# A graph network on one core: padding slots spread over rows, last stage unrolled and its side work moved

## What is computed

```python
x = x + gnn0(layernorm(x), edges, edge_attr)     # per edge: relu(W1 . [x_src, x_dst, attr]); summed per source node
x = x + experts(layernorm(x))                    # shared MLP + top-2 of 4 experts
# two SAGE layers on xn = layernorm(x):
h      = relu(mean_neighbours(xn) @ W_l1 + b1 + xn @ W_r1)
logits = mean_neighbours(h)  @ W_l2 + b2 + h  @ W_r2
x = x + logits
# last block: only the rows with the highest routing weight get the MLP
xn      = layernorm(x)                           # "XN" / "y" in the kernels
weights = xn @ wr + br
top     = the k-1 highest weights (k = half of the 3125 rows, ties by index)
mlp     = gelu(xn @ w1 + b1) @ w2 + b2           # 256 -> 1024 -> 256
x       = x + xn + where(row in top, mlp * weight, 0)
```

## Time and profile before

| | |
|---|---|
| median of the timed runs | 3331.05 us (3328.54 to 3333.71, 3 runs) |
| the profiled execution, its own time | 3306.88 us |
| its span, first to last instruction | 3304.9 us |
| mean granted TensorE clock | 0.865 of 2.4 GHz |
| busy, share of the span | PE 78%, DVE 59%, POOL 55%, PE weight load 44%, ACT 23% |
| DMA | 401.32 MB, mean 121 GB/s |

### The profile page before, as it was taken

The page is one execution under the profiler, slowest core; times in us unless marked ns, Lnnn a source line. Parts: engine busy times, 40 slices in busy tenths (PEclk is TensorE's granted clock), DMA queues, the critical chain, the costliest instruction groups (busy, mean ns, idle before and its releaser), DMA issues. The chain is left out here.

```text
span 3304.9 us, 33972 instructions
## 1 busy us (share of the span) xinstructions
PE 2592.2 (78%) x8449; PEld 1445.8 (44%) x8449; DVE 1966.1 (59%) x4316; ACT 773.9 (23%) x2022; POOL 1819.5 (55%) x1847
## 2 busy tenths in 40 slices
PE   4487784199999899879999877777777777777598
PEld 1133331055544444446666644433334343443476
DVE  7999996377776667514333644444435444444768
ACT  1001010277666666522232300000001000000132
POOL 3777777476665556412100067777754777777310
PEclk8788897599999999989999977788868877777799
DMA  9222220499999999961110033333343333334311
GB/s 256 68 69 82 61 81 13 149 264 263 255 239 234 221 235 234 189 163 49 40 39 9 13 106 105 105 105 105 106 89 101 106 106 105 105 105 103 86 50 41
DMA packets 198569, 401.32 MB, mean 121 GB/s; under 512 B 44315, under 2 KB 93230, under 8 KB 198064
## 3 DMA queue, kind: packets, MB, share of 16 engines
q0 software_dynamic: 93888, 248.27, 31.0%
q1 hardware_dynamic: 98672, 145.05, 13.7%
q10 hardware_dynamic: 5826, 5.93, 0.6%
HBM read 296.76 MB, written 104.52 MB: 121 GB/s over the span
## 5 line engine op out<-in xcount | busy, mean ns | idle before, releaser
L1492 POOL DMA_INDIRECT nbr_yg<-y_d,gidx x878 | 830.1, 945 | 273.0 <-PE nbr_sum L1555 143.6
L1555 PE MATMUL nbr_sum<-nbr_yg,nbr_hot 128*128 128x258 f32 x1756 | 735.3, 534 | 287.3 <-DMA nbr_yg<-y_d,gidx 228.6
L1518 DVE TENSOR_TENSOR nbr<-nbr_sum,nbr 128x258 f32 x878 | 373.5, 425 | 613.4 <-PE nbr_sum L1555 546.7
L1555 PEld LDWEIGHTS nbr_sum<-nbr_yg,nbr_hot 128*128 128x128 f32 x1756 | 367.0, 246 | 643.4 <-DMA nbr_yg<-y_d,gidx 237.7
L704 POOL DMA_INDIRECT qg<-q_d,rb x480 | 470.7, 981 | 322.0 <-DVE hb L787 200.8
L818 PE MATMUL p_sum<-hb,wide 128*96 128x512 f32 x960 | 470.1, 604 | 58.0 <-ACT hb L747 57.1
L362 POOL DMA_INDIRECT recs_d<-recs,slot_src x416 | 403.5, 970 | 152.9 <-issue 135.2
L787 DVE TENSOR_TENSOR hb<-p_h,qg 128x512 f32<-128x512 f32 x480 | 318.3, 684 | 167.1 <-DMA qg<-q_d,rb 156.7
L747 ACT ACTIVATE hb<-hb 128x512 f32<-128x512 f32 x480 | 298.6, 630 | 285.5 <-DVE hb L787 277.5
L566 PE MATMUL acc<-col_hot,lane_hot 128*128 128x440 f16 x832 | 209.9, 419 | 126.8 <-DVE lane_hot L521 126.7
L818 PEld LDWEIGHTS p_sum<-hb,wide 128*96 128x96 f32 x960 | 149.8, 164 | 239.7 <-issue 110.8
(11 more groups left out here) (277 smaller groups left out, 3108.4 us busy)
## 6 DMA issues: line engine op xcount, KB each, us to landing
agg_d<-agg SPq DMA_DIRECT2D x240, 192.4 KB, 5.8
nbr_yg<-y_d,gidx POOLq DMA_INDIRECT x878, 2.7
p_low<-p_d SPq DMA_DIRECT2D x11, 768.0 KB, 13.1
recs_d<-fill SPq DMA_DIRECT2D x16, 510.0 KB, 17.4
rb<-recs_d SPq DMA_DIRECT2D x60, 136.0 KB
qg<-q_d,rb POOLq DMA_INDIRECT x480
recs_d<-recs,slot_src POOLq DMA_INDIRECT x416
agg_d<-no_sums SPq DMA_DIRECT2D x1, 6540.8 KB, 58.5
```

The costliest lines, as they stand in the source:

```text
L1492: pool.indirect_dma_start(yg[t % YB][:, 0:D], None, S.y[:, :], bass.IndirectOffsetOnAxis(ap=C.gidx[:, t:t + 1], axis=0)).then_inc(s_gath[t ...
L1518: dve.tensor_tensor(nbr, p_sum[t % SUMS][:, 0:W], nbr, ALU.add).then_inc(s_acc, 1)
L1555: pe.matmul(p_sum[t % SUMS][:, 0:W], hot[t // BT % HOTS][:, t % BT, :], yg[t % YB][:, :], start=True, stop=True).then_inc(s_sum, 1)
```

## The change

1. **Padding slots.** The slots without an edge no longer all name one row. In `fill` the destination becomes 25 * partition + (0 to 29) by an `iota` instead of 0. In the table `C.gidx` a slot without an edge gets 25 * partition instead of 1600, which takes one more instruction in the prepare stage. Their products still count for nothing.
2. **Neighbour layer 1.** DVE instead of ACT takes the tile xn @ W_r + b from PSUM and adds x2 to it (25 instructions). SP loads the last stage's weights at the layer's start. The reciprocal degrees of the project stage are kept.
3. **Last stage.** The loops are unrolled; `XN` for all tiles stays in SBUF, so that nothing is stored and loaded back; x3 is written over `C.nbr`; PE transposes chunk c+1 between the hidden and the output layer of chunk c; waits of DVE on its own instructions become fewer (three in a tile of the counting stand behind one wait). b2 is not added by POOL: after the gate DVE adds b2 * gate to the residual, 25 instructions, and then combines. Tiles 20 to 24 are taken from PSUM by that last instruction, from a ring of three banks. Semaphores are cleared at the end.

The core of the diff:

```diff
@@ stage_prepare
-                pool.memset(fill[:, :, 1:2].bitcast(U32), 0).then_inc(s_fill, 1)
+                pool.iota(fill[:, :, 1:2].bitcast(I32), [[1, 30]], base=0, channel_multiplier=N_NODES // P).then_inc(s_fill, 1)
+                dve.tensor_scalar(own_row[:, :], C.part_f[:, :], float(NT), float(-NPAD // 2), ALU.mult, ALU.add).then_inc(s_dve, 1)
-                step.link(dve.tensor_scalar(C.gidx[:, :], acc[0][:, 0:NCOL], float(NPAD // 2), None, ALU.add))
+                step.link(dve.tensor_scalar(C.dloc[:, :], acc[1][:, 0:NCOL], 0.0, own_row[:, 0:1], ALU.is_equal, ALU.mult))
+                step.link(dve.scalar_tensor_tensor(out=C.gidx[:, :], in0=acc[0][:, 0:NCOL], scalar=float(NPAD // 2),
+                                                   in1=C.dloc[:, :], op0=ALU.add, op1=ALU.add))
@@ stage_neighbours
+                if layer == 1:
+                    for dst, src in ((C.last_w1[:, :, :], rows_on_partitions(A.w1)), (C.last_b1[:, :], by_feature(A.b1f)),
+                                     (C.last_w2[:, :, :], rows_on_partitions(A.w2)), (C.last_b2[:, :], on_all(A.b2f)),
...
+                        sp.dma_start(dst, src, allow_slow_non_contiguous=True).then_inc(s_last, 16)
-                for tile in range(NT):
+                for tile in range(NT if layer == 0 else 0):
                     act.wait_ge(s_z, tile + 1)
+                    tile, at = divmod(t - 2, EVERY)
+                    if layer == 1 and at == EVERY - 1 and 0 <= tile < NT:
+                        dve.wait_ge(s_z, tile + 1)
+                        dve.tensor_tensor(C.z[:, tile, :], p_z[:, 0:D], C.x2[:, tile, :], ALU.add).then_inc(s_z_taken, 1)
@@ stage_last
-                for c in chunks(sp):
-                    sp.wait_ge(s_ln, LN_STEPS * c + LN_STEPS)
-                    sp.dma_start(chunk(S.xn3, c), y[:, :, :]).then_inc(s_xn_st, 16)
-                    pool.tensor_tensor(r[:, :, :], C.x2[:, bass.ds(c * CH, CH), :], C.z[:, bass.ds(c * CH, CH), :],
-                                       ALU.add).then_inc(s_r, 1)
-                    pool.tensor_tensor(C.nbr[:, bass.ds(c * CH, CH), 0:D], C.nbr[:, bass.ds(c * CH, CH), 0:D],
-                                       b2[:, :, :].to_broadcast([P, CH, D]), ALU.add).then_inc(s_b2, 1)
-                step.link(dve.tensor_scalar(rdeg[:, :, :], C.nbr[:, :, D:D + 1], 1.0, None, ALU.max))
-                step.link(dve.reciprocal(rdeg[:, :, :], rdeg[:, :, :]))
+                    dve.wait_ge(s_dve, counted(max(t - 1, 0)))
...
+                for t in range(NT):
+                    dve.scalar_tensor_tensor(out=C.z[:, t, :], in0=C.last_b2[:, :], scalar=gate[:, t:t + 1], in1=C.z[:, t, :],
+                                             op0=ALU.mult, op1=ALU.add).then_inc(s_z, 1)
+                for t in range(NT):
+                    dve.wait_ge(s_z, t + 1)
+                    if t < CH * LAST:
+                        dve.wait_ge(out.empty, t + 1)
+                        src = C.x2[:, t, :]
+                    else:
+                        src = out.take(dve, t)[:, 0:D]
+                    last = dve.scalar_tensor_tensor(out=C.x2[:, t, :], in0=src, scalar=gate[:, t:t + 1], in1=C.z[:, t, :],
+                                                    op0=ALU.mult, op1=ALU.add)
+                    last.then_inc(s_out, 1)
+                    if t >= CH * LAST:
+                        dve.wait_ge(s_out, t + 1)
+                        dve.sem_inc(out.empty, 1)
```

More of the change, by code:

```diff
@@ L1613, in _ @@
                 sp.dma_start(row[:, :], on_all(S.route[0:N_NODES])).then_inc(s_row_in, 16)
-                for c in chunks(sp):
+                for c in range(NCH):
                     sp.wait_ge(s_out, CH * c + CH)
-                    sp.dma_start(chunk(out_ap, c), C.nbr[:, bass.ds(c * CH, CH), 0:D]).then_inc(s_st, 16)
+                    sp.dma_start(chunk(out_ap, c), C.x2[:, rows(c), :]).then_inc(s_st, 16)
                 sp.wait_ge(s_st, 16 * NCH)
@@ L1632, in _ @@
-                load_ahead(pool, addends, residual)
-                pool.wait_ge(s_w, 64)
-                for c in chunks(pool):
-                    pool.wait_ge(out.empty, CH * c + CH)
-                    pool.tensor_tensor(C.nbr[:, bass.ds(c * CH, CH), 0:D], C.nbr[:, bass.ds(c * CH, CH), 0:D],
-                                       b2[:, :, :].to_broadcast([P, CH, D]), ALU.add).then_inc(s_b2, 1)
+                for c in range(NCH):
+                    pool.wait_ge(s_ln, LN_STEPS * c + LN_STEPS)
+                    pool.tensor_tensor(C.z[:, rows(c), :], C.nbr[:, rows(c), 0:D], XN[:, rows(c), :], ALU.add).then_inc(s_sum, 1)
@@ L1654, in body @@
-                    for t in range(CH):
-                        src = out.to_take(act, c, t)
-                        act.activation(C.nbr[:, bass.ds(c * CH + t, 1), 0:D].rearrange("p a n -> p (a n)"), src[:, 0:D],
-                                       ACT.Copy).then_inc(out.empty, 1)
-                act.wait_ge(s_w, 64)
-                load_xn(0)
-                body(0, False)
-                with act.Fori(1, NCH - 1) as c:
-                    body(c, False)
-                body(NCH - 1, True)
+                                           bias=C.last_b1[:, k:k + 1]).then_inc(hidden.empty, 1)
@@ L1667, in _ @@
+                    if c < LAST:
+                        transposed(c + 1)
+                        for t in range(CH):
+                            src = out.take(act, CH * c + t)
+                            act.activation(C.x2[:, CH * c + t, :], src[:, 0:D], ACT.Copy).then_inc(out.empty, 1)
             @block.vector
             def _(dve):
-                step = Chain(dve, s_deg)
-                step.link(dve.tensor_scalar(rdeg[:, :, :], C.nbr[:, :, D:D + 1], 1.0, None, ALU.max))
-                step.link(dve.reciprocal(rdeg[:, :, :], rdeg[:, :, :]))
@@ L1713, in _ @@
-                step.link(dve.tensor_reduce(rank[:, :], counts[:, :, :], AX.X, ALU.add))
-                step.link(dve.scalar_tensor_tensor(out=gate[:, :], in0=rank[:, :], scalar=float(KEEP), in1=route[:, :],
-                                                   op0=ALU.is_lt, op1=ALU.mult))
-                for c in chunks(dve):
-                    dve.wait_ge(s_b2, c + 1)
-                    for t in range(CH):
-                        tile = bass.ds(c * CH + t, 1)
-                        rows = C.nbr[:, tile, 0:D].rearrange("p a n -> p (a n)")
-                        dve.scalar_tensor_tensor(out=rows, in0=rows, scalar=gate[:, tile],
-                                                 in1=C.z[:, tile, :].rearrange("p a n -> p (a n)"),
-                                                 op0=ALU.mult, op1=ALU.add).then_inc(s_out, 1)
+                        dve.tensor_scalar(spare[:, 0:a], row[:, 0:a], own, None, ALU.is_ge, ALU.add,
+                                          accum_out=counts[:, t, 0:1]).then_inc(s_dve, 1)
@@ new lines, in _ @@
+                    dve.tensor_scalar(spare[:, a:N_NODES], row[:, a:N_NODES], own, None, ALU.is_gt, ALU.add,
+                                      accum_out=counts[:, t, 1:2]).then_inc(s_dve, 1)
+                    dve.scalar_tensor_tensor(out=ties[t % 2][:, 0:b - a], in0=row[:, a:b], scalar=own,
+                                             in1=after[:, 0:b - a], op0=ALU.is_equal, op1=ALU.mult,
+                                             accum_out=counts[:, t, 2:3]).then_inc(s_dve, 1)
+                dve.wait_ge(s_dve, counted(NT))
```

171 lines of the change are left out of this document (83 added, 88 removed).

## The result

| | before | changed |
|---|---|---|
| median of the timed runs | 3332.38 us (4 runs, 3328.54 to 3335.52) | 3200.17 us (4 runs, 3198.67 to 3205.13) |
| ratio, with its 95% interval | | 0.9611 (0.9593 to 0.9630) |
| the profiled execution, its span | 3306.88, 3304.9 us | 3200.9, 3199.6 us |

What follows compares the result with a forecast made beforehand. In the edge network PE was taken to set the pace, with DMA close behind. Terms -72 - 9 + 2 + 1 - 2 = -80 took 3331.05 to 3251 us, range 3234 to 3293.

Steps and rivals of the forecast that it cites:

- Padding, tail and drain: Edge network's end: ten slow padding intervals and the drain shrink to normal pace, 28 us taken.
- Padding, bucket ends: Edge network: gaps every 7 groups from 850 us, 53.6 us, go with cheaper padding; 80% taken, 44 us.
- they sit at the bucket ends: Edge network: the gaps' position, given as the argument against the first rival.
- the first rival: Edge network: DMA near its limit, gaps return with any burst, only the tail's 28 of 72 goes; 3295 us, chance 0.11.
- the ceiling of 83.5: Edge network: most that cheaper padding could save, intervals 21.9, drain 8 and bucket ends 53.6 us.
- Neighbour layers: Both neighbour layers: the last padding tiles no longer delay POOL, -9 us, bounds -7 and -10.
- part 2: Neighbour layer 1: DVE's 25 additions cost nothing, weights load nearly hidden, +2 us, bounds 0 and +10.
- the mark that I had named for a cost: Neighbour layer 1: POOL waiting in the first 20 us would show the forecast wrong.
- Last stage: Last stage: 14.1 us gained early are given back in b2 and the ring wait, -2 us, bounds -8 and +6.
- The 24.2 us between profile and median: Whole kernel: timed median's excess over the profiled execution, kept unchanged in the forecast.
- Theory A: Experiments' expectation, edge network: the repeated row costs more in timed runs than in before's profiled execution; spread rows alone 3212 to 3217.
- Theory B: Experiments' expectation, whole program: the 24 us between median and profile belong to it whatever the rows.
- theory D: Experiments' expectation: the last stage is worth more timed, up to 35 us, than its 12 us profiled.

Runs made afterwards that it cites:

- Spread rows in the old place: Kernel before with spread rows in edge records and neighbour table, DRAM tensors and last stage as before: 3268 us (0.979).
- the kernel with PE not waiting: Changed kernel with output tiles 23 and 24 in the two banks of the transposes: 3529.4 us, last stage 217.3 us.
- set 4: Runs with kernel before at 3587 us; changed kernel with waits behind 74 counts 3540, with tiles 23, 24 in transposes' banks and 15 b2 additions by PE 3521.

## Why the prediction was right and where it was wrong

- **Padding, tail and drain: right.** I took 28 us. With the spread rows alone the last 12 transposes fell from 53.4 to 32.5 us, and from the last transposes to the next stage from 20.4 to 13.9: 27.4 us.
- **Padding, bucket ends: the mechanism was wrong, the size by accident near.** I took 44 us for the gaps that come every 7 groups from 850 us on. Spread rows in the old place leave them whole: 709.1 us up to the last 12 against 705.3. The gaps only lose their rhythm. In the trace of before there are 39 intervals over 3.4 us, ten of them in the tail, and 17 of the other 29 stand at multiples of 7 (groups 70, 77, 91, 98, 112, 119, 133, 140 and on); with spread rows there are 38, none in the tail, anywhere in the second two thirds of the stage. In the old place the transfers fall behind at mid-stage; the padding decided at which group that showed, not how much. The step that failed here is "they sit at the bucket ends", which I held against the first rival. That rival, *bucket ends stay*, because DMA is at its limit late in the stage, was right about the spread rows, and I gave it 0.11. Nor did DMA's share fall from 0.92 to some 0.85: in the changed kernel it is 0.88 to 0.92, since a padding slot is still gathered.
- **What removed those gaps stood in the diff and not in my sum**: `xn3_d` dropped, 3.3 MB lower tensors behind it, 52 to 58 us in this stage (705.3 to 653.7 with one row, 709.1 to 651.3 with spread rows). This is the term that I put at nothing without a reason: I had priced the edit only by its transfers in the last stage. So the edge network gave 84.7 us, 12.7 more than my 72 and 1.2 above the ceiling of 83.5, since both causes went. That the 72 came as near is luck: by themselves the spread rows give this stage 22 to 24 us (779.2 to 755.5, 716.4 to 694.5).
- **Neighbour layers: nearly right.** 9 predicted; -6.4 and -3.1 measured, the second with part 2 in it, and -5.6 and -4.2 with the spread rows alone. Part 2, the weights and additions in layer 1, cost 1.1 us against that kernel's layer (554.8 and 553.7) where I took 2; POOL waited once at the start, 1.78 us, the mark that I had named for a cost. In the kernel with one row and part 2 layer 1 took 4.1 us more than in before (562.0 for 557.9), but layer 0, which has no part 2, 0.7 more too; so the cost lies between 1 and 4.
- **Last stage: mis-sized, -12.0 for -2.** Right: first x3 without the wait, the trip through DRAM (from 3048.22 to 3071.02, 22.8), 10.0 and 8.0 for the instructions behind the gate, the idle of PE (21.28 for about 20) and the lower clock behind it (9.66 us for 32 matmuls that took 7.07 in the kernel with PE not waiting, 2.6 lost where I took 2.5, at a granted clock of 0.50 for the first 3 us), the store (4.6 for 3.9). Too dear: the chunks, 14.3 to 14.4 us where I took 15.2, together 4 us, and above all the counting, 94.8 where I took 102.0, bounds 100.7 to 103.7. I read 0.04 us as a wait's price, the gap between two rows, and did not see that the 0.08 of reading the accumulator would go beside the next count as well. That makes 7 us, and shifts the stage's end by as much, since the ring keeps PE behind the gate.
- **The 24.2 us between profile and median were no constant.** I kept them. Against before's median the spread rows gave 70 us, by stages against its profiled execution 31; all but the spreads gave 105, and 67 by stages. The 38 us missing in both are the gap of before (its median in that set, 3338, over the profiled 3306.9: 31) and the 6 to 8 by which these two kernels' profiled executions lay above their own medians. So before's profiled execution was a quick one, and no other kernel's lay so far under its median. Theory A fits in so far as no such gap is left where either cause is removed (3268 against a profiled 3276, 3233 against 3239), but its figure for the spread rows alone, 3212 to 3217, was missed by over 50 us, before's second profiled execution lay on its median, and no trace of the slower executions exists. Where they lose the time stays open. Theory B is excluded by the changed kernel, whose profiled execution lies on its median. Nothing speaks for theory D: two kernels of set 4 that differ in the last stage alone lie 19.3 us apart when timed and 19.1 by their last stages.
- **Of the Trainium skill's rules**, the one that I weighed (DMA: Bandwidth & Descriptors, "Anatomy of one DMA — SWDGE (gpsimd) path", no term for the address) does not describe these gathers: a packet of the same size took 0.19 to 0.45 us, by rows and by place.
- **Sum.** The profiled executions differ by 106 us, of which I had 80: 13 are missing in the edge network, 10 in the last stage, 3 elsewhere. The other 26 of the 132 come with the median of before. (The small end of my bounds adds up to 45 us and not 44, which changes nothing.)

## What to carry to other kernels

Read a diff for what it allocates, not only for what it executes: a tensor dropped from DRAM moves all behind it, and here that was worth over twice what the visible change to the edge network was (61 to 63 us of that stage against 22 to 24). A rhythm in the stalls tells what triggers them, not what pays for them: ask whether the price of a transfer is raised between the stalls too, which the share of the queue over its packets shows (in the trace of before 0.205 us early and 0.239 from 1150 to 1250 us). And when one profiled execution lies outside the range of its timed runs, don't carry the difference over as a constant.

## What the runs showed of the hardware

- The destination of writes changed the price of the reads that ran beside them: with `agg_d` 3.3 MB higher in DRAM, by the order of declaration, a gather packet took 0.24 to 0.27 us at mid-stage in place of 0.19 to 0.21, and the sums landed in 6.7 and 8.2 us in place of 4.7 and 5.0. The difference is not there at the stage's start: with spread rows in the old place the landing takes 4.7 us from 660 to 760 us, 6.8 from 850 to 950, 8.2 from 1150 to 1250 and 7.4 from 1250 to 1325. The Trainium skill knows a relative of this, in DMA: Bandwidth & Descriptors, "Latency and other measured facts": copies between tensors whose row pitch is a large power of two lose up to half their rate, which it puts down, unverified, to the channels of the memory. No run here shows a pitch, or by which bits of an address this case is slow.
- One row of 2 KB named by all descriptors of a gather costs, at the end of the edge network, 0.45 us a packet in the old place and 0.39 in the new, where spread rows cost 0.22 and 0.19; 30 rows are enough to be rid of it (0.19).
- A wait behind an instruction of DVE that also gives a sum along its row cost 0.12 us in the counting, 0.08 of it the reading of the accumulator, which without the wait starts together with the next instruction. The Trainium skill (VectorE: DVE Perf Modes, "The DRAIN you can't avoid") has a semaphore behind each of eight copies at no cost; for the 74 counts here it was 9.0 us.
- The same program took 3332 to 3338 us in two sets of runs and 3587 to 3623 in four, with pauses of 1 to 4 us in the stages with indirect transfers and in no other; under one chip number there was a set with and a set without them; a comparison in the latter needs a quantity that the pauses leave alone.
